# A gated delta-rule layer with an expert layer on one core: QS joins the second output inside TensorE, level buffers keep their identities, and taps, gathers and scalings stand in another order

## The reference

```python
qkvz = hidden_states @ w_qkvz ; ba = hidden_states @ w_ba
x = silu(depthwise_conv(concat(q, k, v), conv_w))        # 4 taps, causal
beta = sigmoid(b); g = -exp(A_log) * softplus(a + dt_bias)
q = l2norm(q) * DK ** (-0.5); k = l2norm(k)
def step(state, inp):
    state = state * exp(g_t)
    kv_mem = einsum('bhkv,bhk->bhv', state, k_t)
    delta = (v_t - kv_mem) * b_t
    state = state + einsum('bhk,bhv->bhkv', k_t, delta)
    o = einsum('bhkv,bhk->bhv', state, q_t)
xg = out * silu(z)
y = xg * rsqrt(mean(xg * xg) + RMS_EPS) * norm_w ; return y @ w_out
```

## Time and profile before

| what | value |
|---|---|
| median of 3 runs | 3237.49 us (3236.72 to 3246.71) |
| the profiled execution itself | 3209.48 us |
| its span, first to last instruction | 3207.7 us |
| TensorE busy | 2926.0 us, 91% |
| VectorE busy | 2951.7 us, 92% |
| GpSimd busy | 2218.9 us, 69% |
| ScalarE busy | 1798.5 us, 56% |
| granted TensorE clock | 0.975 of full on average |

### The profile page before, as it was taken

The page is one execution under the profiler, slowest core; times in us unless marked ns, Lnnn a source line. Parts: engine busy times, 40 slices in busy tenths (PEclk is TensorE's granted clock), DMA queues, the critical chain, the costliest instruction groups (busy, mean ns, idle before and its releaser), DMA issues.

```text
span 3207.7 us, 56507 instructions
## 1 busy us (share of the span) xinstructions
PE 2926.0 (91%) x18444; PEld 2394.4 (75%) x18444; DVE 2951.7 (92%) x9293; ACT 1798.5 (56%) x4175; POOL 2218.9 (69%) x2394
## 2 busy tenths in 40 slices
PE   7942899999999999999999999999999999999997
PEld 4421678787878877878778877788787787877876
DVE  4997899999999999999999999999999999999996
ACT  3321555565556655565555655566555665656554
POOL 0003677877777777777777777787777777777764
PEclk9975999999999999999999999999999999999999
DMA  2002555555555555555555555555555565555653
GB/s 64 1 1 66 151 142 144 143 149 156 140 146 138 156 151 140 143 141 156 144 146 135 151 157 142 144 138 155 151 145 139 142 159 146 149 134 146 159 143 85
DMA packets 541829, 427.99 MB, mean 133 GB/s; under 512 B 247009, under 2 KB 450785, under 8 KB 541537
## 3 DMA queue, kind: packets, MB, share of 16 engines
q1 hardware_dynamic: 476000, 222.98, 25.6%
q0 software_dynamic: 65536, 201.39, 24.0%
HBM read 345.61 MB, written 45.09 MB: 122 GB/s over the span
## 4 chain that ended last, share of the span: by engine, by line
DVE 62%; PE 22%; ACT 8%; issue 5%; DMA 1%; POOL 1%; POOLq 1%; DVEq 0%; SPq 0%; ACTq 0%
DVE mix L1222 12%; DVE qkv L1181 9%; PE ps L584 4%; DVE E L1169 4%; DVE rows L1201 4%; PE ps L522 3%; DVE xg L1148 3%; PE ps L526 3%; PE ps L556 3%; PE ps L569 3%; PE ps L576 3%; DVE xr L1238 3%; ACT L824 2%; ACT L841 2%; DVE outer L1234 2%
## 5 line engine op out<-in xcount | busy, mean ns | idle before, releaser
L958 POOL DMA_INDIRECT rows<-table,idx_all x1024 | 1200.1, 1172 | 382.7 <-issue 280.3
L813 ACT ACTIVATE qkv<-qkv 128x512 f32<-128x512 f32 x256 | 161.4, 630 | 603.8 <-DVE qkv L1181 603.8
L942 POOL TENSOR_SCALAR xg<-xg,rms 128x128 f32<-128x128 f32 x520 | 407.3, 798 | 7.0
L576 PE MATMUL ps<-XT,E 128*128 128x128 f32 x3072 | 400.5, 277 | 0.0
L556 PEld LDWEIGHTS ps<-X,AT 128*128 128x128 f32 x3072 | 363.4, 192 | 35.7 <-DMA X<-whole 17.9
L1222 DVE SCALAR_TENSOR_TENSOR mix<-rows,zc,mix 128x256 f32<-128x256 f32 x896 | 381.3, 491 | 0.4 <-ACT zc L824 0.4
L556 PE MATMUL ps<-X,AT 128*128 128x128 f32 x3072 | 375.2, 275 | 3.3 <-DMA X<-whole 3.3
L576 PEld LDWEIGHTS ps<-XT,E 128*128 128x128 f32 x3072 | 368.7, 192 | 0.0
L946 POOL COPY gn<-gates 128x8 f32<-128x8 f32 x64 | 12.3, 193 | 481.3 <-SPq L330 262.2
L950 POOL TENSOR_SCALAR gm<-cst,gn 128x128 f32<-128x128 f32 x512 | 340.3, 680 | 6.5
L808 ACT ACTIVATE raw<-ps 128x512 f32<-128x512 f32 x256 | 152.9, 597 | 313.5 <-PE ps L522 313.5
(11 more groups left out here) (165 smaller groups left out, 6172.5 us busy)
## 6 DMA issues: line engine op xcount, KB each, us to landing
Wvz<-wvz SPq DMA_DIRECT2D x64, 512.0 KB, 3.2
xb<-xnT SPq DMA_DIRECT2D x64, 512.0 KB, 4.5
whole<-AT SPq DMA_DIRECT2D x128, 256.0 KB
X<-whole SPq DMA_DIRECT2D x128, 256.0 KB, 4.2
XT<-whole SPq DMA_DIRECT2D x128, 256.0 KB, 4.7
wo<-woh SPq DMA_DIRECT2D x65, 256.0 KB, 4.4
Wkq<-wkq SPq DMA_DIRECT2D x64, 256.0 KB, 2.9
rows<-table,idx_all POOLq DMA_INDIRECT x1024
```

What stands on the lines that cost most here:

```text
L576: done = mm(ps[:, 4 + g, (a % 4) * P:(a % 4 + 1) * P], E[:, a, :], src[:, a, :], start=True, stop=True)
L942: pool.tensor_scalar(xg[:, a, :], xg[:, a, :], rms[:, a:a + 1], None, ALU.mult).then_inc(sm["y_p"], 1)
L958: pool.indirect_dma_start(rows[:, m, :], None, table[:, :], bass.IndirectOffsetOnAxis(ap=idx_all[:, f // 4, c:c + 1], axis=0)).then_inc(ga ...
```

## The change

The diff is cut to its core; the constants, the semaphore lists and `program`'s other buffers follow from it. Buffers `Es` (three, one for each level) hold identities from the start, and each level writes only its new blocks: level 0 by a predicated copy on VectorE, level 1 by ScalarE, level 2 by a copy of half the partitions on VectorE. AT is now the negative triangle without the identity, read straight from bank 6. Y shares its buffer with X. xb is gone.

```diff
@@ TensorE
-                    bank = (7, 6, 7, 6, 7, 6)[u]
+                    bank = (7, 7, 7, 6, 7, 6)[u]
-                                done = mm(ps[...], xb[:, k, t * P:(t + 1) * P],
+                                done = mm(ps[...], xnT[:, k, pn * N + t * P:pn * N + (t + 1) * P],
-                    pe.wait_ge(sm["e_v"], at("e_v", 2 * lv + g + 1))
+                    if lv == 1:
+                        pe.wait_ge(sm["e_s"], at("e_s", 2 * g + 2))
+                    else:
+                        pe.wait_ge(sm["e_v"], at("e_v", lv + g + 1))
                     if lv == 0 and g == 0:
-                        pe.wait_ge(sm["o1_v"], at("o1_v", 1))
+                        pe.wait_ge(sm["xg_v"], at("xg_v", 2))
                     products(0, 6)
-                    pe.wait_ge(sm["tap_s"], at("tap_s", 2))
-                    squares(0, 7)
-                    pe.wait_ge(sm["km_v"], at("km_v", 1))
+                    if back:
+                        pe.wait_ge(sm["x_s"], at("x_s", 2))
+                    squares(0, 3)
                     projection(1)
+                if front:
+                    pe.wait_ge(sm["ssk_v"], at("ssk_v", 1))
...
-                    four(4, 1, lambda b, r, a: MT_b[:, a, :], Y).then_inc(sm["o1_t"], 1)
+                    pe.wait_ge(sm["qs_s"], at("qs_s", 4))
+                    for b in range(2):
+                        for r in range(R):
+                            a, o = task(b, 1, r), (2 * b + r) * P
+                            mm(ps[:, 4, o:o + P], ident, QS[:, b, r * P:(r + 1) * P], start=True, stop=False)
+                            done = mm(ps[:, 4, o:o + P], MT_b[:, a, :], Y[:, a, :], start=False, stop=True)
+                    done.then_inc(sm["o1_t"], 1)
@@ ScalarE
+                def second_level(g):
+                    act.wait_ge(sm["e_t"], at("e_t", 3 + g))
+                    for p0, c0 in ((32, 0), (96, 64)):
+                        A(Es[1][p0:p0 + 32, 4 * g:4 * g + 4, c0:c0 + 32],
+                          ps[p0:p0 + 32, g, :].rearrange("p (a i) -> p a i", a=4)[:, :, c0:c0 + 32], ACT.Copy).then_inc(sm["e_s"], 1)
                     take_XT(0, 1)
+                    second_level(0)
+                    second_level(1)
@@ ScalarE: the four scalings into QS now stand ahead of silu(2), silu_z(0)
@@ GpSimd
-                gather(f, 0)
+                gather(f, 0, 2)
                 if n is not None:
                     finish()
+                gather(f, 2, 4)
...
-                gather(f, 1)
+                gather(f, 4, 8)
...
+            for buf in Es:
+                pool.tensor_copy(buf[:, :, :], mask(C_ID, TASKS)).then_inc(zeroed, 1)
@@ VectorE
-                    V.tensor_tensor(E[:, 4 * g:4 * g + 4, :], ps[:, g, :].rearrange("p (a i) -> p a i", a=4), mask(C_MS + lv, 4), ALU.mult)\
-                        .then_inc(sm["e_v"], 1)
+                    e, new = Es[lv][:, 4 * g:4 * g + 4, :], ps[:, g, :].rearrange("p (a i) -> p a i", a=4)
+                    if lv == 0:
+                        done = V.copy_predicated(e, mask(C_OFF, 4).bitcast(U32), new)
+                    else:
+                        done = V.tensor_copy(e[64:128, :, 0:64], new[64:128, :, 0:64])
+                    done.then_inc(sm["e_v"], 1)
...
-                        st.did(V.scalar_tensor_tensor(out=AT[:, a, :], in0=km[:, a // R, :], scalar=scol[:, a:a + 1], in1=DT[:, a, :],
-                                                      op0=ALU.mult, op1=ALU.mult))
-                    st.wait()
-                    V.tensor_tensor(AT[:, 4 * g:4 * g + 4, :], AT[:, 4 * g:4 * g + 4, :], mask(C_ID, 4), ALU.add).then_inc(sm["at_v"], 1)
+                        V.scalar_tensor_tensor(out=AT[:, a, :], in0=ps[:, 6, (a // R) * P:(a // R + 1) * P], scalar=nscol[:, a:a + 1], in1=DT[:, a, :],
+                                               op0=ALU.mult, op1=ALU.mult).then_inc(sm["at_v"], 1)
...
-                    second_outputs()
+                    gated(1, ps[:, 4, :], rq2[nx], z2[nx])
                     level(0, 0)
                     level(0, 1)
-                    expert_mix(0)
+                    expert_mix(0, 2)
+                if front:
+                    for d in (1, 2, 3):
+                        tap(0, d)
+                if back:
+                    expert_mix(2, 4)
...
-                    second_gated(nx)
-                    level(1, 0)
-                    level(1, 1)
...
+                if back:
+                    scaled_y(0, 1, "y0_t", "ys0_v")
                 if front:
...
-                    eliminate(0, 4)
-                if back:
-                    scaled_y(0, 1, "y0_t", "ys0_v")
-                if front:
-                    eliminate(4, HB - 1)
+                    eliminate(0, HB - 1)
```

More of the change, by code:

```diff
@@ L66, in constants @@
     p, j = i[:, None], i[None, :]
-    def level(n):
-        off = (p // (2 * n) == j // (2 * n)) & (p // n == j // n + 1)
-        return np.eye(P) - off
+    off = (p // (2 * BL) == j // (2 * BL)) & (p // BL == j // BL + 1)
     eye = np.broadcast_to(np.eye(BL).reshape(1, BL * BL), (P, BL * BL))
-    m = [np.eye(P), p <= j, p > j, p < j, eye[:, :P], eye[:, P:]] + [level(n) for n in LEVELS]
+    m = [np.eye(P), p <= j, p > j, eye[:, :P], eye[:, P:], off]
     m = np.stack([np.asarray(a, np.float32) for a in m], 1).reshape(P, NC * P)
@@ L279, in program @@
         XT = sb("XT", [P, TASKS, P])
-        E = sb("E", [P, TASKS, P])
-        Y = E
+        Es = [sb(f"E{lv}", [P, TASKS, P]) for lv in range(len(LEVELS))]
+        Y = X
         RV = sb("RV", [P, TASKS, P])
@@ L525, in projection @@
                             for k in range(KD):
-                                done = mm(ps[:, bank, (t % 2) * 256:(t % 2) * 256 + 256], xb[:, k, t * P:(t + 1) * P],
+                                done = mm(ps[:, bank, (t % 2) * 256:(t % 2) * 256 + 256], xnT[:, k, pn * N + t * P:pn * N + (t + 1) * P],
                                           Wvz[:, k, 2 * P:4 * P], start=k == 0, stop=k == KD - 1)
@@ L805, in take @@
                         act.wait_ge(sm["conv_v"], last("conv_v", u + 3))
-                    bank = (7, 6, 7, 6)[u]
+                    bank = (7, 7, 7, 6)[u]
                     w = cwkq[:, u, 3:4] if u < 2 else cwv[:, u - 2, 3:4]
@@ L902, in one_pass @@
                               scale=cols_b[:, 1, a:a + 1]).then_inc(sm["qs_s"], 1)
+                if front:
+                    silu(2)
+                    silu_z(0)
+                if back:
                     act.wait_ge(sm["out_t"], at("out_t", 2))
@@ L950, in gate_sums, with gather @@
                     pool.tensor_scalar(gm[:, a, :], mask(C_LE), gn[:, a:a + 1], None, ALU.mult).then_inc(sm["gm_p"], 1)
-            def gather(f, hf):
-                for k in range(hf * (K // 2), (hf + 1) * (K // 2)):
+            def gather(f, k0, k1):
+                for k in range(k0, k1):
                     for s in range(2):
@@ L1205, in expert_dots, with expert_mix @@
                                     half_of(prob_all[:, n // 4, (n % 4) * 16:(n % 4) * 16 + 16], hf), ALU.mult).then_inc(sm["dot_v"], 1)
-                def expert_mix(hf):
-                    dve.wait_ge(sm["silu_e"], at("silu_e", hf + 1))
-                    for k in range(hf * (K // 2), (hf + 1) * (K // 2)):
+                def expert_mix(k0, k1):
+                    dve.wait_ge(sm["silu_e"], at("silu_e", k0 // 4 + 1))
+                    for k in range(k0, k1):
                         for s in range(2):
@@ L1237, in eliminate @@
                         v = x[:, :, j + 1:HB, 0:m]
-                        last_row[0] = st.did(V.tensor_tensor(v, v, o, ALU.subtract))
+                        last_row[0] = st.did(V.tensor_tensor(v, v, o, ALU.add))
                 def lower_products():
@@ L1315, in one_pass @@
                         dve.wait_ge(sm["o1_t"], last("o1_t"))
-                        dve.wait_ge(sm["qs_s"], last("qs_s"))
-                    second_outputs()
+                    gated(1, ps[:, 4, :], rq2[nx], z2[nx])
                     level(0, 0)
                     level(0, 1)
-                    expert_mix(0)
-                    st.wait()
-                    dve.sem_inc(sm["half_v"], 1)
+                    expert_mix(0, 2)
                 if front:
@@ L1326, in one_pass @@
                 if back:
-                    second_gated(nx)
-                    level(1, 0)
-                    level(1, 1)
+                    expert_mix(2, 4)
+                    st.wait()
+                    dve.sem_inc(sm["half_v"], 1)
                     if place["u"]:
@@ L1379, in one_pass @@
                 if front:
-                    for d in (1, 2):
-                        tap(3, d)
+                    for d in (1, 2, 3):
+                        tap(2, d)
+                if front:
+                    tap(3, 1)
                 if back:
@@ L1384, in one_pass @@
                 if front:
-                    tap(3, 3)
+                    for d in (2, 3):
```

(1 more changed line is left out.)

67 lines of the change are left out of this document (25 added, 42 removed).

## The result

The kernel before took 3238.51 us in this comparison (3236.72 to 3246.71), the changed one 3192.43 us (3186.1 to 3217.81, four runs): a ratio of 0.9871, 95% interval 0.9831 to 0.9912. That is 1.3% faster, clear of the noise but small: 46 us where 116 were forecast. Both kernels ran again on a later chip: 3215.33 and 3188.75 us, ratio 0.9909 (0.9877 to 0.9941). The changed kernel repeats to 4 us, the kernel before moves by 23 us from one comparison to the next; no run shows why. The two profiled executions stand close to the later pair: 3209.5 before, 3198.7 after, 10.8 us apart. So the forecast was missed on either count.

What follows compares the result with a forecast made beforehand. TensorE and VectorE both nearly full; TensorE's need of 41.7 to 42.3 plus 0.90, taken as 42.7, plus 0.27 gives 43.0 a pass. Gain 1.8 times 63 plus 2 is 116 us: 3121 us, range 3083 to 3198.

Steps and rivals of the forecast that it cites:

- the one on DMAs: Blocks' way out and back between xrT and its reader: room goes from 8.7 to 8.4 us, 0.1 a pass allowed.
- The step on the second stall: TensorE's 0.92 us wait for scaled_y(0) goes, with 0.7 to spare; GpSimd ends its pass at the same place.
- the stalls only move: Rival: each wait removed comes back elsewhere and the added 0.9 is just met; pass 44.8, 3236 us, chance 0.05.
- The joint: Rival: VectorE reaches scaled_y(1), needed by the last product, 0.7 to 1.5 us late; 3170 to 3210 us, chance 0.22.
- The list of signs: Signs of being right, such as a pass of about 43 us, and of being wrong, such as longer X<-whole waits.
- Three stalls: TensorE's stalls of 1.10, 0.92 and 0.26 us a pass, together 2.28, were all to go.
- VectorE 4.6 us less: Removed and shortened VectorE operations take its work from 42.3 to 37.7 us a pass.
- ScalarE's narrow copies: Four added ScalarE instructions on 32 partitions x 128: 1.2 us at most, 0.6 if narrow ones are half, hidden.
- TensorE 0.90 more: Four identity products, eight instructions, add 0.90 us a pass on TensorE, with nothing to hide it.
- The slower rival: Added bank-4 identity products don't pipeline: eight take 3.7 us instead of 0.90, pass 45.8, 3300 us, chance 0.09.
- The rule weighed: VectorE's change of starting partition at the third level holds the first dots 0.08 us; 5 us over 63 passes, left out.
- Outside the loop: First pass's identity copies fit GpSimd's idle time, shorter triangles gain, last pass swaps an addition for products: -2 us for both.

Runs made afterwards that it cites:

- the version with gathers deferred and MT late: Kernel after with the last four gathers issued in the next pass and VectorE's two MT products behind the last tap: 3086.22 us, later 3077.02 us.

## Why the prediction was wrong, point by point

**The step that failed is the one on DMAs**, which said: "That is a little tighter; I allow 0.1 a pass." It took the 8.7 us between xrT and its reader for a slot into which the blocks' trip fits, and checked that the slot shrank by only 0.3. The trip itself was taken as fixed, and for it the sum got 0.1 us a pass where it cost 1.9. It was 8.1 us long in the kernel before, 0.6 less than the slot, and the change made it longer: 9.8 us by the landings, 9.99 until TensorE starts. The step on the second stall says that "GpSimd ends its pass at the same place", while the stalls removed ahead of the elimination (1.10 us and the small waits) let xrT come earlier. Counted from the first X products of that pass, xrT ends at 34.5 us, before at 35.9, and GpSimd's eight gathers start at 29.0, before at 28.8. So 1.4 gathers more start behind xrT. The prediction had both facts and didn't set them beside each other. That late gathers are what makes the trip bind is shown by leaving them out and by deferring four; through which of them the store ends later is not shown. The wait for X in the kernel after is 87.3 / 63 = 1.4 us a pass, and the pass without late gathers is 44.59 - 42.67 = 1.9 us shorter, nearly the whole forecast gain of 1.8. Of the rivals, "the stalls only move" named the round trip, "2 us late", with a chance of 0.05 and 3236 us. The joint's 3185 us is near the time measured, but by another mechanism, and it is only because the joint's case was taken into the range of 3083 to 3198 us that the first time, 3192, lies in it: luck. The list of signs was better than the forecast: a longer wait for X<-whole stood there among the signs of being wrong.

The other steps:
- *Three stalls.* All gone, as said: no product of TensorE waits for the silu, for the scaled solution ahead of Kd's, or for RV. Only the weight loads of L581 still wait for the scaled solution, 15.1 us in 63 passes, and no product stands for it.
- *VectorE 4.6 us less.* 4.05 less by the busy times of one pass. The predicated copy took 0.73 us, forecast 0.69, bounds 0.37 to 1.07. The 64x256 copy took 0.43, not 0.37 (it reads PSUM and the row that priced it SBUF; no run tells whether that is why). Eight triangles from PSUM took 2.15 us, no more than from SBUF. By groups, of the kernel after:

```profile
L1177 DVE COPY_PREDICATED E<-cst,ps 128x512 f32<-128x512 uint32 x126 | 91.6, 731 | 73.0 <-PE ps L550 72.9
...
L829 ACT ACTIVATE E<-ps 32x128 f32<-32x128 f32 x252 | 67.8, 269 | 6.2
...
L1179 DVE COPY E<-ps 64x256 f32<-64x256 f32 x126 | 53.8, 427 | 88.3 <-PE ps L550 88.3
```

- *ScalarE's narrow copies.* Four took 1.15 us (0.27 busy each), as much as four of 128 partitions: the upper bound of 1.2, and hidden.
- *TensorE 0.90 more.* Held: sixteen products at 0.12 us each, no wait between an opening product and the one that adds to it. The slower rival never came near. TensorE's need of 42.6 to 43.2 held too, at 42.67 without late gathers.
- *The joint.* The chain from the third level to xrT was forecast at 18.3 us and took 18.46. The tie was real: it shows as soon as the trip is out of the way, at 0.29 us a pass, below the 0.7 to 1.5 of its rival.
- *The rule weighed.* The copy of the third level at partition 64 starts at 1024.50 and takes 0.43 us; the dots behind it, at partition 0, start at 1024.96, after its end, while each of the mixes costs 0.42 in its row. The rule of the Trainium skill, "VectorE: DVE Perf Modes", section "Two Vector instructions with no wait between them", says just that, and the trace agrees. It is worth less than 0.1 us a pass.
- *Outside the loop.* Forecast 2 us less. The profiled times less 63 passes leave 387.7 us before and 389.5 after: some 2 us more, which is about what this difference can tell.
- *From the profile to the runs.* Taking the profiled gain off the median carried the 28 us between them along as if it were fixed. It isn't: the kernel after runs below its profiled time (3192 and 3189 against 3198.7).

## What to carry to other kernels

When stalls are taken out, the engines' chains get shorter but an engine that was not on them can keep its place in time, and its DMAs slide further over transfers of the others. So a transfer that is waited for in 3 passes of 63 need not have room to spare; this one had 0.6 us, and it grew by 1.7. Put its length, its slot and its traffic into the sum, and list for each stretch which other DMAs will now start in it, and when. Traffic that nobody needs soon (here rows wanted half a pass later) can be issued where no trip is under way, and here that was worth more than the change itself.

## What the runs showed that was not expected

- Leaving out the eight late gathers gained nothing in the kernel before and 1.9 us a pass in the kernel after; moving four of them into the next pass gained 1.5.
- The trip does not go by the number of gathers alone. Without any behind xrT the load of X started 2.60 us behind it and X was whole at 6.63 us. With 2.0 started in the 9 us behind xrT (two runs) the load started at 4.0 and X came at 7.9; with 2.7 in the kernel before, at 2.9 and 8.1; with 2.9 in the version with gathers deferred and MT late, at 3.9 and 8.8; with 4.0 to 4.3 (five traces), at 4.0 to 4.1 and 9.8. (Means over the passes, from the semaphore events.)
- Four gathers more ahead of a scaling left TensorE standing for about 3 us 56 times in some 62 passes, with VectorE and ScalarE idle beside it in the stall shown, and the clock fell behind it. Each stall of 3 us cost 1 us more by the clock.
- Four ScalarE copies of 32 partitions x 128 took 1.15 us, four of 128 x 128 take 1.16.
